# A low product of 64 stationary columns moves behind the first of every three transposes, in a fused graph-attention layer

## The reference, cut to what matters

```
q = x @ wq.T + bq;  k = x @ wk.T + bk;  v = x @ wv.T + bv
q2, k2, v2 = (second projections of q, k, v), each split into 16 heads of 64
scores = einsum('hnd,hmd->hnm', q2, k2) / 8 + mask        # mask from 6144 edges
attn   = softmax(scores)
out    = einsum('hnm,hmd->hnd', attn, v2)                 # heads joined to (N, 1024)
y      = layernorm(x + out @ wo.T + bo)
```

## Time and profile before

| | |
|---|---|
| three runs | 297.44, 297.70, 297.91 us, median 297.7 |
| profiled execution, its own time | 297.57 us |
| its span, first to last instruction | 295.8 us |
| PE busy / PEld busy | 98% / 93% of the span |
| DVE / ACT / POOL busy | 68% / 59% / 48% |
| chain that ended last | PE 96%, DVE 1%, ACT 1% |
| granted TensorE clock | 0.995 of full speed over the span |

### The profile page before, as it was taken

How to read it: one execution, slowest core, us unless ns; L and a number is a source line. 1 busy time by engine, 2 the same in 40 slices (tenths; PEclk the granted TensorE clock), 3 DMA queues, 4 the chain that set the end, 5 groups by cost and what they waited for, 6 DMA issues and landing times.

```text
span 295.8 us, 5260 instructions
## 1 busy us (share of the span) xinstructions
PE 289.2 (98%) x1640; PEld 274.3 (93%) x1640; DVE 200.8 (68%) x494; ACT 175.9 (59%) x331; POOL 141.3 (48%) x124
## 2 busy tenths in 40 slices
PE   8999999999999999999999999999999999999992
PEld 8999999999999998888999999999999998888882
DVE  4879977667766774204468798888888888833184
ACT  4863234433443352421298999999999999934432
POOL 2000635545555552659955354636372727845600
PEclk9999999999999999999999999999999999999998
DMA  7979556443662438826211303121222222410013
GB/s 220 377 237 334 190 190 191 139 156 131 213 214 91 131 135 334 306 73 196 97 38 63 115 16 129 48 94 54 88 70 71 71 71 71 161 55 0 2 71 142
DMA packets 14318, 39.83 MB, mean 135 GB/s; under 512 B 3200, under 2 KB 4832, under 8 KB 14176
## 3 DMA queue, kind: packets, MB, share of 16 engines
q1 hardware_dynamic: 12192, 38.38, 37.6%
q0 software_dynamic: 1680, 0.62, 1.1%
q10 hardware_dynamic: 432, 0.66, 0.8%
HBM read 37.44 MB, written 2.21 MB: 134 GB/s over the span
## 4 chain that ended last, share of the span: by engine, by line
PE 96%; DVE 1%; ACT 1%; issue 0%
PE bank L900 21%; PE bank L891 19%; PE bank L893 19%; PE bank L892 19%; PE bank L998 6%; PE bank L981 5%; PE bank L967 3%; PE bank L971 3%; PE bank L909 2%; DVE h_lo L793 0%; ACT h_hi L499 0%; ACT res L576 0%; ACT h_hi L394 0%; DVE att_sum L767 0%; DVE stats L865 0%
## 5 line engine op out<-in xcount | busy, mean ns | idle before, releaser
L337 POOL DMA_INDIRECT mask_cells<-cell_value,cell x48 | 53.6, 1117 | 75.1 <-DMA mask_cells<-cell_value,cell 31.3
L308 POOL TENSOR_TENSOR w_lo<-w_raw,w_hi 128x1024 fp32r<-128x1024 f32 x20 | 47.6, 2405 | 42.9 <-DVE probs L786 38.8
L891 PE MATMUL bank<-x_hi,w_hi 128*128 128x384 f32 x192 | 64.3, 335 | 0.0
L893 PE MATMUL bank<-x_hi,w_lo 128*128 128x384 f32 x192 | 64.1, 334 | 0.0
L892 PE MATMUL bank<-x_lo,w_hi 128*128 128x384 f32 x192 | 64.1, 334 | 0.0
L394 ACT ACTIVATE w_hi<-w_raw 128x1024 fp32r<-128x1024 f32 x50 | 52.4, 1054 | 19.3 <-PE bank L900 13.6
L440 ACT ACTIVATE h_hi<-bank,bcol 128x384 f32 (+1 forms) x24 | 14.0, 581 | 57.0 <-PE bank L893 57.0
L891 PE MATMUL bank<-h_hi,w_hi 128*128 128x384 f32 x128 | 46.4, 362 | 0.0
L603 DVE TENSOR_TENSOR w_lo<-w_raw,w_hi 128x1024 fp32r<-128x1024 f32 x30 | 36.6, 1223 | 12.5 <-ACT w_hi L394 10.2
L893 PE MATMUL bank<-h_hi,w_lo 128*128 128x384 f32 x128 | 43.0, 336 | 0.0
L892 PE MATMUL bank<-h_lo,w_hi 128*128 128x384 f32 x128 | 42.9, 335 | 0.0
(11 more groups left out here) (104 smaller groups left out, 530.6 us busy)
## 6 DMA issues: line engine op xcount, KB each, us to landing
w_raw<-weights SPq DMA_DIRECT2D x54, 512.0 KB
probs<-key_rows SPq DMA_DIRECT2D x6, 512.0 KB
res<-x_rows SPq DMA_DIRECT2D x1, 1536.0 KB, 6.7
out<-res SPq DMA_DIRECT2D x6, 256.0 KB, 2.0
v<-x_t SPq DMA_DIRECT2D x6, 192.0 KB, 5.7
w_raw<-weights SPq DMA_DIRECT2D x3, 256.0 KB, 4.2
mask_cells<-cell_value,cell POOLq DMA_INDIRECT x48
mask_cells<-mask SPq DMA_DIRECT2D x1, 576.0 KB, 4.4
```

The costliest lines, as they stand in the source:

```text
L308: nc.gpsimd.tensor_tensor(lo, w_raw[:, s, cols], hi.bitcast(F32), ALU.subtract)\
L337: nc.gpsimd.indirect_dma_start(out=mask_cells, out_offset=bass.IndirectOffsetOnAxis(ap=cell[:, c:c + 1], axis=0), in_=cell_value[:, c:c + ...
L891: pe.matmul(out_ps, w_hi[:, s, cols], moving_hi, start=(k == 0), stop=False)
L893: return pe.matmul(out_ps, w_lo[:, s, cols], moving_hi, start=False, stop=(k == KT - 1))
```

## The change

The low products leave `values`. `high_product` is what stays (both heads 128 stationary columns); `low_product` now has 64 stationary columns for both heads and is issued inside `transposes`, between the first transpose of a group and the other two. The even head's low products (g = 0 to 2) go with T(3) to T(5) of the same step, the odd head's (g = 3 to 5) wait for T(0) to T(2) of the next step; their low weights get a buffer of their own, `pt_odd`. In `vp` the block of zeros and the second copy of the odd head's high part are dropped. In ACT's and DVE's queues the work on the odd head's output moves back: `att_half_out(a - 1, 1)`, `att_high(a - 1)` and `add_halves(a - 1, 1)`. In the tail the low products of pair 6 stay beside the high ones; those of pair 7, groups 0 to 3, go inside T(2) to T(5).

```diff
@@ buffers
-        vp = sb("vp", [P, 2, NT, 6 * D], F32R)
-        EVEN_HIGH, EVEN_LOW, ODD_LOW, ODD_HIGH, ZERO, ODD_AGAIN = range(6)
+        pt_odd = sb("pt_odd", [P, NT, N], F32R)
+        def pt_lo(g):
+            return h_lo[:, V0 + 4 + g, :] if g < NT else pt_odd[:, g - NT, :]
+        vp = sb("vp", [P, 2, NT, 4 * D], F32R)
+        HIGH, LOW = range(2)
@@ POOL, v_low
-                nc.gpsimd.tensor_copy(v_slots(par, ODD_AGAIN - 1, ODD_AGAIN)[:, :, 1, :],
-                                      highs[:, :, 1, :].bitcast(F32)).then_inc(vp_done, 1)
@@ ACT, pt_high
-                    if g >= NT:
-                        act.wait_ge(pv_done, 2 * NT * a + (g - NT + 1))
+                    if not (isinstance(a, int) and a == 0 and g < NT):
+                        act.wait_ge(pv_hi_done, 2 * NT * a + (g - NT + 1))
@@ ACT, step
                     v_high(a, 1 - par)
-                    if not (isinstance(j, int) and j < 2):
-                        att_half_out(a - 1, 1)
                     exps(a, range(0, 5))
...
                         pt_high(a, (2 + h,))
                     double(par, h)
-                if not (isinstance(j, int) and j < 2):
-                    att_high(a - 1)
+                    if h == 0 and not (isinstance(j, int) and j < 2):
+                        att_half_out(a - 1, 1)
                 if attend:
                     pt_high(a, (4, 5))
+                if not (isinstance(j, int) and j < 2):
+                    att_high(a - 1)
                 evacuate(t + 1, L1_TILES + 1 + 2 * j, par, 1)
@@ DVE, attention
                 pt_low(a, (1,))
-                if not (isinstance(a, int) and a == 0):
+                if last:
                     add_halves(a - 1, 1)
                 pt_low(a, (2,))
                 if u is not None:
                     evacuate_pair(u, par, 0)
+                if not (last or isinstance(a, int) and a == 0):
+                    add_halves(a - 1, 1)
                 pt_low(a, (3,))
@@ PE
-            def transposes(a, g):
+            def transposes(a, g, between=None):
                 for b in range(NT):
                     ins = pe.transpose(...)
+                    if b == 0 and between is not None:
+                        low_product(*between)
...
+                pe.matmul(out_bank[h][:, 0:N], vp[:, par, m, 2 * h * D:2 * (h + 1) * D], pt_hi[:, g % 3, :],
+                          start=(m == 0), stop=(m == NT - 1)).then_inc(pv_hi_done, 1)
+            def low_product(a, par, g):
+                h, m = divmod(g, NT)
+                pe.matmul(out_bank[h][0:D, 0:N], vp[:, par, m, 2 * h * D:(2 * h + 1) * D], pt_lo(g),
+                          start=False, stop=True, skip_group_check=True).then_inc(pv_done, 1)
@@ PE, step
-                            if more and KT - VALUES_FROM + k < 2 * NT:
-                                values(a - 1, par, KT - VALUES_FROM + k)
+                            if more and k < NT:
+                                high_product(a - 1, par, NT + k)
...
-                                values(a, 1 - par, k - VALUES_FROM)
-                            if 0 <= k - TRANSPOSES_FROM < 2 * NT:
-                                transposes(a, k - TRANSPOSES_FROM)
+                                high_product(a, 1 - par, k - VALUES_FROM)
+                                transposes(a, k - TRANSPOSES_FROM, (a, 1 - par, k - VALUES_FROM))
+                            elif k >= TRANSPOSES_FROM:
+                                transposes(a, k - TRANSPOSES_FROM,
+                                           (a - 1, par, NT + k - TRANSPOSES_FROM) if more else None)
```

More of the change, by code:

```diff
@@ L158, in v_pair, with v_slots @@
             return v2[:, :, ds(a * P, P)].rearrange("p n (h d) -> p n h d", h=2)
-        def v_slots(par, first, last):
-            step = last - first
-            return vp[:, par, :, :].rearrange("p n (z d) -> p n z d", z=6)[:, :, first:last + 1:step, :]
+        def v_slots(par, which):
+            return vp[:, par, :, :].rearrange("p n (h z d) -> p n h z d", h=2, z=2)[:, :, :, which, :]
         raw_loaded = [sem(f"raw_loaded{s}") for s in range(RING)]
@@ L482, in v_high @@
             def v_high(a, par):
-                nc.scalar.activation(v_slots(par, EVEN_HIGH, ODD_HIGH), v_pair(a), ACT.Copy).then_inc(vp_hi_done, 1)
+                nc.scalar.activation(v_slots(par, HIGH), v_pair(a), ACT.Copy).then_inc(vp_hi_done, 1)
             def exps(a, tiles=range(2 * NT)):
@@ L527, in step @@
                     double(par, h)
+                    if h == 0 and not (isinstance(j, int) and j < 2):
+                        att_half_out(a - 1, 1)
+                if attend:
+                    pt_high(a, (4, 5))
                 if not (isinstance(j, int) and j < 2):
                     att_high(a - 1)
-                if attend:
-                    pt_high(a, (4, 5))
                 evacuate(t + 1, L1_TILES + 1 + 2 * j, par, 1)
@@ L593, in _ @@
             nc.vector.memset(zeros[:, :], 0.0).then_inc(consts_dve, 1)
-            nc.vector.memset(vp[:, :, :, ZERO * D:(ZERO + 1) * D].bitcast(F32), 0.0).then_inc(acc_free, 2)
-            nc.vector.memset(mask[:, :, :], NEG)
+            nc.vector.memset(mask[:, :, :], NEG).then_inc(acc_free, 2)
             def low_part(t, s):
@@ L792, in pt_low @@
                     dve.wait_ge(pt_hi_done, 2 * NT * a + (g + 1))
-                    nc.vector.tensor_tensor(pt_lo[:, g % 3, :], pt_bank(a, g)[:, 0:N],
+                    if not (isinstance(a, int) and a == 0):
+                        dve.wait_ge(pv_done, 2 * NT * (a - 1) + (g + 1))
+                    nc.vector.tensor_tensor(pt_lo(g), pt_bank(a, g)[:, 0:N],
                                             pt_hi[:, g % 3, :].bitcast(F32), ALU.subtract)\
@@ L1066, in _ @@
             project(0, 0, left)
-            for g in range(KT - VALUES_FROM, 2 * NT - 1):
-                values(a - 1, 0, g)
+            for g in range(NT, 2 * NT - 1):
+                high_product(a - 1, 0, g)
+                low_product(a - 1, 0, g)
             project(0, 1, left)
-            values(a - 1, 0, 2 * NT - 1)
+            high_product(a - 1, 0, 2 * NT - 1)
+            low_product(a - 1, 0, 2 * NT - 1)
             pe.wait_ge(acc_free, L1_TILES + 2 + 2 * PAIRS)
@@ L1091, in _ @@
             for g in range(4):
-                values(a, 1, g)
-                transposes(a, g + 2)
+                high_product(a, 1, g)
+                transposes(a, g + 2, (a, 1, g))
                 project(*((1, 3), (0, 4), (1, 4), (0, 5))[g])
-            values(a, 1, 4)
+            high_product(a, 1, 4)
+            low_product(a, 1, 4)
             project(1, 5)
-            values(a, 1, 5)
+            high_product(a, 1, 5)
+            low_product(a, 1, 5)
             pe.wait_ge(sum_done, 2 * a + 1)
```

15 lines of the change are left out of this document (8 added, 7 removed).

## The result

The changed kernel takes 301.51 us (median of 4 runs, 301.40 to 301.61) against 297.68 of before: 3.8 us slower, ratio 1.0126 with a 95% interval of 1.0114 to 1.0138. The direction of the forecast holds and the size doesn't: I had 1.9 us, and 301.5 lies above the range.

A forecast was written before the change was run, and what follows sets the result against it. PE's own stream was taken as the bound, with a chain T(1), ACT, DVE, scores 0.24 us behind. Saving zero, waits 1.70 + 0.16 + 0.07 = 1.93 us: 297.7 + 1.9 = 299.6 us; own range 299.0 to 300.3, whole range 295.4 to 300.7.

The forecast's parts named there:

- The change on PE: Low products behind the first transpose on PE: saving taken as zero, with 2.3 us over 43 places as other end.
- One of the readings that led there: Rows at 170.62: a 128-column transpose load on an idle loader was taken to last 0.06 to 0.07, not 0.11.
- The rule that spoke against me: Skill's 56 ns for a 128-column matmul: with 64-column loads behind transposes, 43 places would save some 2.2 us.
- the prediction's lower bound: att_half_out in ACT's gapless stretch was to add between 0.37 and 0.52 us.
- point 2 of "The change on the chain behind PE": ACT's gapless stretch: att_half_out adds 0.37 to 0.52, att_high nothing; tile 1 leaves ACT at 207.87 to 208.02, before 207.15.
- 0.24 of slack: PE's time to spare at the first score load, between tile 1 emptied by DVE and the load at 208.33.
- the tail, which I had at 0.07: Tail: the chain 0.58 later, PE 0.52, so 0.07 more than the 0.16 PE already waited there.
- point 3, DVE by itself: DVE: add_halves ahead of pt_low(3) adds 0.58; tile 1 emptied at 208.63, a score wait of 0.34 per step.
- the last rival: Longer chain: upper bounds of the copy and DVE's waits give 0.5 per step, 2.9 in all, 300.6 us; chance 0.07.
- the same 0.34: PE's forecast wait per step ahead of the scores for tile 1's emptying, full price in steps 3 to 7.
- The upper end of the range: Whole range of the forecast time reached up to 300.7 us; the forecast's own range ended at 300.3.

The follow-up runs named there:

- e1: Changed kernel with each low product ahead of its three transposes instead of behind the first; 301.64 us, ratio 1.0131.
- e2: Kernel of before with the even head's 64-column low products behind the first transpose of T(3) to T(5); 297.58 us against 297.88, ratio 0.9991.
- e6: Changed kernel with the score products in blocks 4, 5, 6 of tile 0 instead of 3, 4, 5; 300.63 us, ratio 1.0091.
- e3: Changed kernel with att_high on ACT moved from behind pt_high(5) to between pt_high(4) and pt_high(5); 300.57 us, ratio 1.0094.
- e5: Changed kernel with att_high on ACT moved behind tile 1's evacuation; 300.52 us, ratio 1.0098.
- e12: Kernel of before with att_high on ACT moved behind pt_high(4) and pt_high(5); 298.92 us against 297.68, ratio 1.0045.
- e13: Kernel of before with the odd head's add_halves on DVE moved behind tile 0's evacuation, ahead of pt_low(3); 300.66 us against 297.68, ratio 1.0099.
- e4: Changed kernel without the semaphore waits on pt_high and pt_low that the queues' order implies; 301.86 us, ratio 1.0127.
- e11: Changed kernel with the odd head's low products back in blocks 0 to 2 and ACT's and DVE's orders as before; 297.68 us, ratio 1.0001.

## Why the prediction was right and wrong

**Right: the saving is zero.** Section "The change on PE" took the transpose in front, not the loader, as what sets the 0.11. The changed trace shows 0.11 with a 64-column load behind a transpose, and e1 and e2 find no time in the place. One of the readings that led there is weaker than I made it: a load that starts 0.06 behind a transpose's load on an idle loader (170.62, 170.69) need not be that load's duration, for in e6, where such a load had waited 0.27, the next one (of 64 columns) starts 0.01 behind it (215.55, 215.56). The rule that spoke against me, 56 ns for a matmul of 128 columns in "TensorE: Matmul & The Clock Gate" of the Trainium skill, section "Back-to-back issue gap", doesn't hold for these transposes: 0.11 here. The section gives the 56 ns for a matmul by itself and 81 ns for 128 columns in a stream with loads, which the prediction passed over; the transposes here take more than either.

**Right: the mechanism of the loss.** PE's own stream is unchanged and tile 1 is emptied too late for the scores: the wait stands where I put it, and the step grows. `att_half_out` adds the 0.37 of the prediction's lower bound: `pt_high(3)` starts at 205.62, 4.84 behind T(0), and before at 203.74, 4.03 behind it, 0.81 more; 0.44 of this is there at `pt_high(1)` already (1.82 behind T(0), before 1.38), 0.36 from the later T(1) and 0.08 from the doubled wait.

**Wrong: its size.** The step that failed is point 2 of "The change on the chain behind PE": "`att_high` only changes places inside the stretch: nothing." I had found no idle time on ACT from `pt_high(1)` to the evacuation and took the stretch as a sum in which order doesn't matter. But it has a second anchor, T(5), which moves 0.52 back. Work ahead of `pt_high(5)` can hide while T(5) isn't there; work behind it is paid in full. `att_high` went from the one side to the other: 0.52 more on ACT between T(5) and the evacuation (0.98 for 0.46). So ACT starts on tile 1 1.04 later against T(0) (7.31 for 6.27), where the prediction had 0.72 to 0.87.

A smaller term was off too. The prediction let DVE end 0.04 + 0.63 = 0.67 behind ACT, counted from ACT's second half. DVE starts 0.70 behind ACT's start (208.79, 208.09) and takes 1.25 for its two halves against ACT's 1.16, so it ends 0.79 behind. The sum by what was measured: 1.04 on ACT; DVE 0.89 behind ACT before (208.04, 207.15) and 0.79 now (210.04, 209.25), 0.10 less; 0.24 of slack off. That leaves 0.70, against 0.34 forecast and 0.69 measured. Five steps with 0.33 more each are 1.7 us of the 1.9 that were missing, and most of the rest is the tail, which I had at 0.07 and which showed 0.40: there too ACT's evacuation starts 1.05 later behind T(0).

How much of it is `att_high`? e3 and e5 give back 0.9 and 1.0 us when it is moved, and e12 loses 1.2 with nothing else changed. In e5 the scores come 0.26 sooner in the step and still 0.43 later than before, where point 3, DVE by itself, had 0.34. So point 3 held within 0.1 (it had no lag for the doubled waits), and the 0.26 on top of it is what `att_high`'s place costs. e5 gives back less than 0.26 in every step would, as in two steps PE then waits for the mask.

**Half right: `pt_low(3)`.** The prediction named this wait in the last rival as "part of the same 0.34". In the changed kernel that holds, since the later wait for tile 1 covers it. But alone, DVE's moved `add_halves` is the dearest of the edits: 3.0 us in e13, part of which is `att_high` on ACT waiting for it, a dependence that the prediction didn't name. The costs overlap and don't add (1.2 and 3.0 alone, 3.8 with the products' move), because a late `pt_low(3)` and a late tile 1 hold up the same queue, and time lost at the first is no longer lost at the second.

**The upper end of the range** came from adding up the durations' upper ends; it held no case with a mistake in the order. That is why 301.5 fell outside.

**Not settled.** Why the transpose takes 0.11: kernels with half the moving or half the stationary columns in the transposes would show it and weren't tried. `att_half_out`'s part alone wasn't separated on the chip; its 0.37 is read from the trace. Nor was the place of the odd low products with both queues as before, so how much of the 1.5 us it would cost by itself is open.

## What to carry to other kernels

A stretch without gaps on an engine is not free to be reordered: mark in it every instruction that waits for the bounding engine, and count what stands behind each such anchor separately, for what moves from ahead of an anchor to behind it is paid in full on that engine even if the sum stays, and the bounding engine loses what its slack doesn't cover (in e12 a copy of 0.5 us, some 0.2 us in each step). Before a delay is built to gain a better place, measure the place alone (e2: one small edit, no gain); here that was the whole promise, and the delay cost 3.8 us. And before an instruction leaves a spot where its engine waits anyway, look at what it pushes back and at who reads its result: 0.56 us of DVE moved out of such a gap cost 3.0, as PE waited for the next `pt_low` and ACT for the sum.

## What the runs showed of the hardware

- A 128x128 transpose of float32 holds PE for 0.11 us at a granted clock of 1.00, whether the load behind it has 64 columns (206.45 to 206.56 in the changed kernel, 204.04 to 204.15 in e2) or 128 (T(0) to T(5) before, 0.11 apart).
- An ordinary load of 128 columns takes 0.11 and one of 64 columns 0.06, as the section "LDWEIGHTS (loading the stationary operand)" of the page "TensorE: Matmul & The Clock Gate" of the Trainium skill has it. The rows of a transpose's load don't fit it: they are recorded with 0.14, like a load of 64 columns (0.13), and a next load can start 0.06 behind.
- The recorded 0.27 of a transpose and 0.33 of a product are not their share of PE's time: transposes that follow each other start 0.11 apart, products 0.17. The spacing of starts tells what a matmul costs, but not from a transpose to the product right behind it, whose row begins 0.02 behind (206.45, 206.47); there the loads or the sum over both tell it.
- One more semaphore to wait for makes `pt_high` start 0.12 behind its transposes instead of 0.04 (e4 against the changed kernel). Where the engine has slack or an anchor further on, it costs no time (e4 and e11).
